# A depthwise 5x5 convolution on one core: every strip's top square alone in a PSUM bank, 15 tiles a channel instead of 13

## The reference

```python
k = jnp.transpose(kernel, (1, 2, 0))[:, :, None, :]
y = lax.conv_general_dilated(x, k, window_strides=(1, 1), padding='SAME',
        dimension_numbers=('NHWC', 'HWIO', 'NHWC'), feature_group_count=ch)
return x + y
```

## Time and profile before

| | |
|---|---|
| median of 3 runs | 811.67 us (811.26 to 812.08) |
| the profiled execution: its time, its span | 809.37 us, 807.5 us |
| busy: PE, DVE, ACT, POOL | 99%, 83%, 80%, 63% of the span |
| share of PE in the chain that ended last | 98% |
| granted TensorE clock | 0.999 |
| time that packets took of the 16 DMA engines' span | 97.7% |

### The profile page before, as it was taken

The page is one execution under the profiler, slowest core; times in us unless marked ns, Lnnn a source line. Parts: engine busy times, 40 slices in busy tenths (PEclk is TensorE's granted clock), DMA queues, the critical chain, the costliest instruction groups (busy, mean ns, idle before and its releaser), DMA issues.

```text
span 807.5 us, 19118 instructions
## 1 busy us (share of the span) xinstructions
PE 799.7 (99%) x6929; PEld 797.6 (99%) x6929; DVE 666.4 (83%) x2581; ACT 647.9 (80%) x1445; POOL 511.5 (63%) x194
## 2 busy tenths in 40 slices
PE   8999999999999999999999999999999999999997
PEld 7999999999999999999999999999999999999997
DVE  7888878888888888788888878888888888788875
ACT  6878888887878888887878888887878888887875
POOL 2766665757666665757566665757566666757563
PEclk9999999999999999999999999999999999999999
DMA  9999999999999999999999999999999999999965
GB/s 372 420 407 397 393 389 399 391 397 401 388 398 397 385 410 385 397 405 388 391 401 392 400 390 397 406 389 394 394 394 404 386 403 390 398 396 390 394 263 235
DMA packets 32494, 313.36 MB, mean 388 GB/s; under 512 B 3600, under 2 KB 6800, under 8 KB 8080
## 3 DMA queue, kind: packets, MB, share of 16 engines
q1 hardware_dynamic: 31968, 311.67, 97.7%
q10 hardware_dynamic: 432, 0.46, 0.2%
HBM read 161.13 MB, written 150.99 MB: 387 GB/s over the span
## 4 chain that ended last, share of the span: by engine, by line
PE 98%; DMA 1%; SPq 0%; DVE 0%; ACT 0%; issue 0%; DVEq 0%
PE sums L455 86%; PE sums L444 7%; PE sums L442 4%; DMA x_in<-x 1%; SPq L292 0%; DVE x_low L264 0%; ACT x_high L325 0%; ACT y_out L333 0%; DVE taps_split L241 0%; DVE y_out L365 0%; DVEq L169 0%
## 5 line engine op out<-in xcount | busy, mean ns | idle before, releaser
L455 PE MATMUL sums<-weights,x_high 121*128 121x226 f32 (+3 forms) x4224 | 718.0, 276 | 0.0
L455 PEld LDWEIGHTS sums<-weights,x_high 121*128 121x128 f32 x4224 | 640.9, 192 | 0.0
L264 POOL TENSOR_TENSOR x_low<-x_in,x_high 121x1920 fp32r<-121x1920 f32 x95 | 411.7, 4334 | 277.6 <-ACT x_high L325 277.6
L455 PE MATMUL sums<-weights,x_low 121*128 121x196 f32 (+3 forms) x2112 | 574.2, 272 | 2.0 <-DVE x_low L264 1.4
L333 ACT ACTIVATE y_out<-sums 128x220 f32<-128x220 f32 (+6 forms) x1248 | 390.7, 371 | 148.4 <-PE sums L455 139.7
L455 PEld LDWEIGHTS sums<-weights,x_low 121*128 121x128 f32 x2112 | 405.5, 192 | 2.6 <-issue 1.8
L325 ACT ACTIVATE x_high<-x_in 121x1920 fp32r<-121x1920 f32 (+1 forms) x195 | 295.0, 1513 | 5.2 <-DMA x_in<-x 5.1
L264 DVE TENSOR_TENSOR x_low<-x_in,x_high 121x1280 fp32r<-121x1280 f32 (+1 forms) x100 | 222.0, 2223 | 71.6 <-ACT x_high L325 71.6
L371 DVE TENSOR_TENSOR y_out<-sums,y_out 128x96 f32<-128x96 f32 (+3 forms) x1056 | 263.1, 249 | 10.2 <-ACT y_out L333 0.3
L365 DVE TENSOR_TENSOR y_out<-sums,y_out 128x44 f32<-128x44 f32 (+2 forms) x768 | 150.0, 195 | 31.8 <-ACT y_out L333 31.7
L259 POOL TENSOR_TENSOR weights<-taps_split,places_in 121x450 fp32r<-121x450 f32 x95 | 103.9, 1094 | 7.1 <-DVE taps_split L247 7.1
(11 more groups left out here) (11 smaller groups left out, 4.3 us busy)
## 6 DMA issues: line engine op xcount, KB each, us to landing
x_in<-x SPq DMA_DIRECT2D x95, 1600.0 KB, 12.1
y<-y_out SPq DMA_DIRECT2D x95, 1536.0 KB, 8.3
taps_in<-taps SPq DMA_DIRECT2D x22, 150.0 KB, 12.2
x_in<-x SPq DMA_DIRECT2D x5, 320.0 KB, 5.2
y<-y_out SPq DMA_DIRECT2D x3, 302.5 KB, 2.9
y<-y_out SPq DMA_DIRECT2D x1, 357.5 KB, 3.6
taps_in<-taps ACTq DMA_DIRECT2D x2, 150.0 KB, 4.8
y<-y_out SPq DMA_DIRECT2D x1, 271.0 KB, 2.4
```

The costliest lines, as they stand in the source:

```text
L264: engine.tensor_tensor(x_low[slot][0:SQUARE, cols], x_in[c % X_SLOTS][0:SQUARE, cols], x_high[slot][0:SQUARE, cols].bitcast(F32), ALU.subt ...
L455: product = pe.matmul(sums, v[slot][0:SQUARE, at:at + IMAGES], window, start=n == 0 and v is x_low, stop=n == len(squares) - 1 and part == ...
```

## The change

`TILES` now gives every strip the tiles (0), (1, 2), (3, 4), the outer ones too: 15 tiles a channel. The step that adds a row seam waits for all of DVE's steps on the tile before. `wait_bank` waits for DVE's step after a tile with a square alone too. POOL waits for DVE's piece of `x_low` before it places the taps of the same channel. ACT makes the second piece of `x_high` behind tile 2 of a channel (before: behind the second strip), and in channel 0 the pieces come behind tiles 4 and 7; DVE's `x_low` piece and taps step in channel 0 come behind tile 4. At the start, the mask, the unit taps and the first four channels' taps come in one transfer (`start`), only channel 0's taps are split ahead of the first windows and the other three channels' behind the second strip's `x_low`, the zeros are 128 columns read four times, and 15 products of zeros are made instead of 17.

```diff
-TILES = tuple((j, squares) for j in range(GRID) for squares in (
-    ((0, 1), (2, 3, 4)) if SUM_COLS[j][1] == EDGE else ((0,), (1, 2), (3, 4))))
+TILES = tuple((j, squares) for j in range(GRID) for squares in ((0,), (1, 2), (3, 4)))
...
-ZERO_COLS = 512
-ZERO_PRODUCTS = 17
+ZERO_REPEATS = 4
+ZERO_PRODUCTS = 15
...
+HIGH_AT = (0, 3)
+FIRST_HIGH_AT = (5, 8)
...
-            load_taps(act, 0)
-            act.dma_start(places_in[:, :], places).then_inc(places_loaded, 16)
+            act.dma_start(start_in[:, :], start).then_inc(start_loaded, 16)
             load_taps(act, 1)
...
             for c in range(CHANNELS):
-                for piece, (_, end) in enumerate(LATER_PIECES):
-                    if c < LAST:
-                        split_high(c + 1, piece)
-                    for i in range(len(TILES)):
-                        if LATER_PIECES[piece][0] <= TILES[i][0] < end:
-                            copy_sums(c, i)
+                places = HIGH_AT if c else FIRST_HIGH_AT
+                for i in range(len(TILES)):
+                    if i in places and c < LAST:
+                        split_high(c + 1, places.index(i))
+                    copy_sums(c, i)
...
                 if row_seam(i):
+
+                    dve.wait_ge(y_step, stepped(c, i - 1))
                     seam = y[:, first:first + SEAM]
                     dve.tensor_tensor(seam, sums[:, 0:SEAM, FRESH_AT[j]:FRESH_AT[j] + FRESH[j]], seam,
                                       ALU.add).then_inc(y_step, 1)
...
             for step in range(SPLIT_STEPS):
-                split_taps(dve, 0, step)
+                split_taps(dve, 0, 0, 1, step)
             place_taps(dve, 0)
             for piece in range(len(pieces_of(0))):
                 split_low(dve, 0, piece, low_by_dve)
+                if piece == 1:
+                    for step in range(SPLIT_STEPS):
+                        split_taps(dve, 0, 1, BATCH, step)
             for c in range(CHANNELS):
-                if c < LAST:
-                    split_low(dve, c + 1, 0, low_by_dve)
-
-                if c % BATCH < SPLIT_STEPS and c // BATCH + 1 < BATCHES:
-                    split_taps(dve, c // BATCH + 1, c % BATCH)
                 for i in range(len(TILES)):
+                    if i == (HIGH_AT if c else FIRST_HIGH_AT)[0]:
+                        if c < LAST:
+                            split_low(dve, c + 1, 0, low_by_dve)
+
+                        if c % BATCH < SPLIT_STEPS and c // BATCH + 1 < BATCHES:
+                            split_taps(dve, c // BATCH + 1, 0, BATCH, c % BATCH)
                     finish_sums(c, i)
...
             for c in range(1, CHANNELS):
+
+                pool.wait_ge(low_by_dve[c % SLOTS], lows(c, 0))
                 place_taps(pool, c)
                 split_low(pool, c, 1, low_by_pool)
...
-                if row_seam(before) or col_seam(before):
+                if row_seam(before) or col_seam(before) or alone(before):
                     pe.wait_ge(y_step, stepped(c + back, before))
```

More of the change, by code:

```diff
@@ L142, in lows, with split_steps @@
     return before + sum(by_dve(c, p) == mine for p in range(piece + 1))
+def split_steps(c):
+    return SPLIT_STEPS * (1 if c == 0 else c // BATCH + 2)
 def summed(c, i):
@@ L165, with build @@
 LAST_STORES = tuple((Y_AT[j], Y_AT[j + 1] if j < GRID - 1 else Y_COLS) for j in range(GRID))
-def build(nc, x, taps, places, out):
+def build(nc, x, taps, start, out):
     with ExitStack() as ctx:
@@ L183, in build @@
         weights = [sbuf(f"weights{i}", [P, 2, PART_COLS], F32R) for i in range(SLOTS)]
-        zeros = sbuf("zeros", [P, ZERO_COLS], F32R)
-        places_in = sbuf("places_in", [P, TAP_COLS + TURNED_COLS], F32)
+        zeros = sbuf("zeros", [P, P], F32R)
+        start_in = sbuf("start_in", [P, (BATCH + 1) * TURNED_COLS + TAP_COLS], F32)
         warm = sbuf("warm", [P, 1], F32)
         psum = ctx.enter_context(nc.psum_tensor("sums", [P, BANKS, BANK], F32))
-        (zeros_ready, warm_zeroed, warmed, weights_zeroed, margins_zeroed, places_loaded,
+        (zeros_ready, warm_zeroed, warmed, weights_zeroed, margins_zeroed, start_loaded,
          taps_step,
          tile_summed, tile_copied, y_step) = (sems(n, 1)[0] for n in (
-             "zeros_ready", "warm_zeroed", "warmed", "weights_zeroed", "margins_zeroed", "places_loaded", "taps_step",
+             "zeros_ready", "warm_zeroed", "warmed", "weights_zeroed", "margins_zeroed", "start_loaded", "taps_step",
              "tile_summed", "tile_copied", "y_step"))
@@ L227, in load_taps, with given_taps, split_taps @@
                              ).then_inc(taps_loaded[slot], 16)
[L229 to L234, removed]
-            if step == 0:
-                engine.wait_ge(taps_loaded[batch % TAPS_SLOTS], 16 * (uses(batch, TAPS_SLOTS) + 1))
+        def given_taps(batch):
+            if batch == 0:
+                return start_in[0:SQUARE, 0:BATCH * TURNED_COLS].rearrange("p (c n) -> p c n", n=TURNED_COLS)
+            return taps_in[batch % TAPS_SLOTS][0:SQUARE, :, :]
+        def split_taps(engine, batch, first, end, step):
+            slot, count = batch % SPLIT_SLOTS, end - first
+            given = given_taps(batch)[:, first:end, :]
+            high, low = (taps_split[slot][0:SQUARE, first:end, part, :] for part in (HIGH, LOW))
+            left = rest[slot][0:SQUARE, first:end, :]
+            at = BATCH * TURNED_COLS
+            centre = start_in[0:SQUARE, at:at + TURNED_COLS].unsqueeze(1).broadcast_to([SQUARE, count, TURNED_COLS])
+            if step == 0:
+                if batch == 0:
+                    engine.wait_ge(start_loaded, 16)
+                else:
+                    slot_uses = uses(batch, TAPS_SLOTS) + (batch % TAPS_SLOTS > 0)
+                    engine.wait_ge(taps_loaded[batch % TAPS_SLOTS], 16 * slot_uses)
                 if batch >= SPLIT_SLOTS:
@@ L241, in split_taps @@
                 engine.tensor_tensor(high, given, centre, ALU.add).then_inc(taps_step, 1)
-            elif step == 1:
-                engine.wait_ge(taps_step, SPLIT_STEPS * batch + 1)
-                engine.tensor_tensor(left, high.bitcast(F32), centre, ALU.subtract).then_inc(taps_step, 1)
-            else:
-                engine.wait_ge(taps_step, SPLIT_STEPS * batch + 2)
-                engine.tensor_tensor(low, given, left, ALU.subtract).then_inc(taps_step, 1)
+            else:
+                engine.wait_ge(taps_step, split_steps(batch * BATCH + first) - SPLIT_STEPS + step)
+                if step == 1:
+                    engine.tensor_tensor(left, high.bitcast(F32), centre, ALU.subtract).then_inc(taps_step, 1)
+                else:
+                    engine.tensor_tensor(low, given, left, ALU.subtract).then_inc(taps_step, 1)
         def place_taps(engine, c):
@@ L252, in place_taps @@
             turned = taps_split[batch % SPLIT_SLOTS][0:SQUARE, c % BATCH, :, :].bitcast(F32).unsqueeze(2).broadcast_to(shape)
-            mask = places_in[0:SQUARE, 0:TAP_COLS].rearrange("p (a n) -> p a n", n=TURNED_COLS).unsqueeze(1).broadcast_to(shape)
+            mask = start_in[0:SQUARE, (BATCH + 1) * TURNED_COLS:].rearrange("p (a n) -> p a n", n=TURNED_COLS).unsqueeze(1).broadcast_to(shape)
             windows = weights[slot][0:SQUARE, :, TAP_AT:TAP_AT + TAP_COLS].rearrange("p w (a n) -> p w a n", n=TURNED_COLS)
-            engine.wait_ge(taps_step, SPLIT_STEPS * (batch + 1))
+            engine.wait_ge(taps_step, split_steps(c))
             if c >= SLOTS:
@@ L281, in reload_taps @@
                 if batch >= TAPS_SLOTS:
-                    sp.wait_ge(taps_step, SPLIT_STEPS * (batch - TAPS_SLOTS + 1))
+                    sp.wait_ge(taps_step, split_steps((batch - TAPS_SLOTS + 1) * BATCH - 1))
                 load_taps(sp, batch)
@@ L400, in _ @@
             pool.wait_ge(weights_zeroed, SLOTS)
-            pool.wait_ge(places_loaded, 16)
+            pool.wait_ge(start_loaded, 16)
             for c in range(1, CHANNELS):
+                pool.wait_ge(low_by_dve[c % SLOTS], lows(c, 0))
                 place_taps(pool, c)
@@ L462, in _ @@
             for n in range(ZERO_PRODUCTS):
-                pe.matmul(psum[:, 0, :], zeros[:, 0:P], zeros[:, :], start=True, stop=True)
+                pe.matmul(psum[:, 0, :].rearrange("p (a n) -> p a n", n=P), zeros[:, :],
+                          zeros[:, :].unsqueeze(1).broadcast_to([P, ZERO_REPEATS, P]), start=True, stop=True)
             for c in range(CHANNELS):
@@ L517 @@
     arrays = {"x": lay_out_input(np.asarray(x)), "taps": np.ascontiguousarray(turned),
-              "places": np.concatenate([lay_out_mask(), lay_out_taps(unit)[0]], axis=1)}
+              "start": np.concatenate([turned[0], lay_out_taps(unit)[0], lay_out_mask()], axis=1)}
     nc = bacc.Bacc("TRN2", target_bir_lowering=False, num_devices=1)
```

1 line of the change is left out of this document (removed).

## The result

The changed kernel takes 852.29 us, the median of 4 runs (851.96 to 852.50), against 811.88 us (811.26 to 812.16) for the kernel before on the same chip: 1.051 times as long, with a 95% interval of 1.0495 to 1.0524. The profiled execution took 852.27 us, its span is 850.5 us. The forecast was 857 us, in a range of 843 to 873.

The account below looks back on a forecast made before the run. DVE was to replace PE as the bound: 12.1 + 96 x 7.05 + 95 x 1.41 + 69 x 0.38 = 849.1 us, span 852.5, 45 more than before, so 811.7 + 45 = 857 us, range 843 to 873.

Parts of the forecast that it names:

- What bounds the kernel: DVE becomes the bound with 8.73 us a channel on average, against PE's 8.15 to 8.175.
- the signs that the prediction named: In the profile after: DVE at 97% or more, PE idle before its bank waits about 0.6 us a channel.
- The price of a wait: At ten row seams a channel, DVE starts 0.105 us after its predecessor's end; bounds 0.035 and overlap as before.
- The strips: DVE's finishing steps, start to start: middle strip 1.56 us, first 0.85, last 1.52; 7.05 us a channel.
- the reason I gave, POOL's wait: DVE's step after `x_low` comes 1.41 us later because POOL waits for `x_low`; 0.8 us a channel given back.
- The start: PE begins real work near 8.1 us; DVE's first finishing step comes near 12.1, bounds 11.5 and 13.
- The sum: DVE's start, strips, `x_low` and taps steps: 12.1 + 676.8 + 134.0 + 26.2 = 849.1 us; span 852.5.
- its two reasons: 31 intervals between DVE's starts each 1.5% off (13 us), and the start 1 us: 843 to 873.
- the step from the profiled execution to the median: The runs' median lies 2.3 us above the profiled execution, so 811.7 + 45 = 857 us.
- PE as the bound after all: DVE's sum falls below PE's 8.15 us a channel, as with seams at 0.035; 800 us median; chance 0.06.
- The taps step that meets POOL: POOL gets ahead of DVE's taps step, which waits 0.79 us in 69 channels: 54 us, 911; chance 0.05.
- PE's gain: Outer strips' wide product of 364 columns costs 0.17 to 0.185 us; PE's channel takes 0.08 to 0.11 less.

## Why the prediction was right

**What bounds the kernel.** Right. PE's 8.255 us gave way to a channel on DVE. Between two `x_low` starts lie mostly 8.74 to 8.77 us in a channel with a taps step and 8.36 to 8.40 without, where 8.84 and 8.46 were forecast; the mean over 94 channels is 8.69, forecast 8.73. One of the signs that the prediction named did not come: DVE shows 85% busy and not 97%, because the places where it waits for itself are not counted. And PE waits longer than 0.15 us in 72 channels, not in each, 0.4 us there on average for the 0.6 named.

**The price of a wait.** It rested on one row of the kernel before, two L371 in 0.62 us, and held in 960 places: 0.105 us after the predecessor's end, 0.035 with one semaphore. The experiments with the needed and the swapped waits show both as causes and not only as durations. The rule of the Trainium skill (VectorE: DVE Perf Modes, "The DRAIN you can't avoid"), that semaphores between chained VectorE operations cost nothing extra, does not hold for these steps: the kernel with the same 31 steps a channel takes 800 or 852 us by what they wait for and in which order.

**The strips.** 1.56, 0.85 and 1.52 us were forecast, 1.53, 0.87 and 1.50 came. The steps with 96 and 104 elements last 0.25 and 0.26 instead of 0.26 and 0.27, which I had not foreseen. `x_low` with 1.40 for 1.41 was right in size; the reason I gave, POOL's wait, was only one of two that each do it, and without it ACT's earlier piece would have given the same 1.40. That part was right by luck.

**The start.** PE's first real product came at 8.08 (8.1 forecast), DVE's first finishing step at 11.95 (12.1).

**The sum.** DVE's last step ended at 847.1, forecast 849.1. The strips, 7.05 us a channel in the forecast, took about 6.98, which is 7 us less in all, and `x_low` 1 us less; 5.2 us of pauses (below) and about 0.8 us of waits in the first two channels were missing. That errors of 8 and 6 us nearly cancel is luck; either alone would have stayed inside the range. The range itself is not the one that its two reasons give: 13 and 1 us around 857 end at 871, not 873. The rest of the 5 us between 857 and 852.3 is mostly the step from the profiled execution to the median: I added the 2.3 us by which the three runs of before lay above their profiled one, and here the two agree within 0.1.

**The rivals.** PE as the bound after all came with 800 us, in the kernels where the condition named for it was made true, DVE's sum under PE's 8.15 with a seam at 0.035: 800.42. The taps step that meets POOL did not come, but only because POOL waits: with that wait alone taken out it came, in ten channels, with 4.1 us and not the 0.79 I had priced. I had looked at POOL's short placing as the one that gets in, not at its large piece behind it.

**PE's gain.** The wide product of 364 columns costs what that of 392 costs, or nearly: an outer strip is 1.63 us, at the upper end of 1.62 to 1.635.

## What to carry to other kernels

Before work is moved to an engine that is "83% busy", lay its steps out start to start and count which of them wait for their own predecessor; here a wait for the step just ahead cost 0.12 us (the overlap of 0.085 and a gap of 0.035), and a second semaphore on that instruction 0.07 more where it was the one served last. Wait for the step that really wrote the data, and issue that wait first. Steps like `x_low` and the splitting of the taps, on VectorE with both inputs in SBUF, must not be allowed to race a long one on GpSimd: here the loser paid 4.1 us for a winner of 4.2, and TensorE's clock on top where the stall reached it.

The kernel with only the needed waits beats both: 0.987 of before, 0.939 of the change (799.99 / 852.29; by the two ratios to before it is the same).

## What was not expected of the hardware

In the changed kernel DVE pauses at regular places. This row of its timeline shows one; the wait is put down to ACT, but that copy had ended 2.3 us earlier, at 70.87.

```profile
73.15 0.20 DVE L385 TENSOR_TENSOR y_out<-sums,y_out 128x36 f32<-128x36 f32 x1 [0.46 <-ACT y_out L353]
```

After 25 us there are fifteen gaps like it, of 0.18 to 0.47 us, and five smaller delays, and nowhere else does DVE start more than 0.025 us later than is usual between the same two instructions. Between any two of the twenty lie 128 instructions of DVE's queue, those that only wait included, or a multiple of it. Such places are 25.6 to 26.4 us apart, and 11 of the 31 show no pause. Together they make up 5.2 us of the span, and the same 5.2 us in the kernel with the late piece of ACT. That the queue is filled in pieces of 128 would explain it; nothing here was done to test that, and it stays open.
